# Second expert products of the last unit as three 16-bit products, with the splits on POOL and DVE

## The reference

```
x = x + 0.5 * ffn(layernorm(x))
x = x + attn(layernorm(x))
x = x + 0.5 * ffn(layernorm(x))
```

```
h = relu(einsum('ebnc,ech->ebnh', buf, W1) + b1)     # 128 -> 512
y = einsum('ebnh,ehc->ebnc', h, W2) + b2             # 512 -> 128
```

## Time and profile before

| | |
|---|---|
| median of 3 runs | 190.1 us (189.92 to 190.57) |
| the profiled execution | 190.01 us |
| its span, first to last instruction | 188.2 us |
| PE busy | 178.3 us (95%) |
| ACT busy | 150.9 us (80%) |
| DVE busy | 135.0 us (72%) |
| POOL busy | 66.1 us (35%) |
| granted TensorE clock | 1.0 in all slices |

### The profile page before, as it was taken

The page is one execution under the profiler, slowest core; times in us unless marked ns, Lnnn a source line. Parts: engine busy times, 40 slices in busy tenths (PEclk is TensorE's granted clock), DMA queues, the critical chain, the costliest instruction groups (busy, mean ns, idle before and its releaser), DMA issues.

```text
span 188.2 us, 5958 instructions
## 1 busy us (share of the span) xinstructions
PE 178.3 (95%) x2279; PEld 142.0 (75%) x2279; DVE 135.0 (72%) x402; ACT 150.9 (80%) x362; POOL 66.1 (35%) x106
## 2 busy tenths in 40 slices
PE   7998799999999999999999999898999999999991
PEld 7976798888978956654756565554699998999980
DVE  0998967957978799795557768799787785354254
ACT  3795999659869779999999999799887489885670
POOL 8924842000040007776654778579200000000000
PEclk9999999999999999999999999999999999999999
DMA  4999930360005999617875973704500008300303
GB/s 126 323 332 332 207 60 0 74 125 0 3 2 171 254 218 279 212 64 185 252 229 153 242 191 79 207 6 84 101 0 3 0 3 140 69 5 28 86 3 111
DMA packets 36460, 23.35 MB, mean 124 GB/s; under 512 B 16424, under 2 KB 33360, under 8 KB 36432
## 3 DMA queue, kind: packets, MB, share of 16 engines
q1 hardware_dynamic: 35744, 22.70, 48.4%
q10 hardware_dynamic: 688, 0.27, 0.5%
HBM read 14.05 MB, written 5.24 MB: 102 GB/s over the span
## 4 chain that ended last, share of the span: by engine, by line
PE 80%; DVE 13%; issue 4%; ACT 1%; DVEq 0%; POOL 0%; ACTq 0%; POOLq 0%
PE psB L1080 19%; PE psB L1155 7%; PE psS L960 5%; PE psS L962 5%; PE psS L961 5%; PE psB L1056 5%; PE psS L1138 4%; PE psB L970 4%; PE psB L1157 3%; PE psB L1047 3%; PE psB L1022 3%; DVE oh L860 2%; PE psB L1087 2%; PE psB L960 2%; PE psB L1176 2%
## 5 line engine op out<-in xcount | busy, mean ns | idle before, releaser
L604 POOL TENSOR_SCALAR_AFFINE_SELECT amat<-amat 128x512 f32<-128x512 f32 x64 | 44.7, 705 | 35.1 <-ACT amat L700 33.5
L700 ACT ACTIVATE amat<-psS 128x768 f32<-128x768 f32 x64 | 48.7, 815 | 3.1 <-PE psS L1140 2.3
L658 ACT ACTIVATE hid<-psS,biasT 128x160 f32<-128x160 f32 x128 | 39.4, 404 | 6.3 <-PE psS L962 5.5
L1080 PE MATMUL psB<-hid,w 128*128 128x160 f32 x256 | 39.6, 303 | 1.4 <-issue 1.3
L1080 PEld LDWEIGHTS psB<-hid,w 128*128 128x128 f32 x256 | 35.5, 190 | 2.5 <-issue 2.0
L960 PE MATMUL psS<-xe,w 128*128 128x160 f16 x128 | 27.1, 233 | 0.4 <-DVE xe L355 0.3
L962 PE MATMUL psS<-xe,w 128*128 128x160 f16 x128 | 27.1, 233 | 0.0
L961 PE MATMUL psS<-xe,w 128*128 128x160 f16 x128 | 27.1, 233 | 0.0
L670 ACT ACTIVATE yT<-psB,biasT 128x160 f32<-128x160 f32 (+1 forms) x32 | 13.4, 438 | 9.5 <-PE psB L1080 9.3
L1155 PE MATMUL psB<-amat,vst 128*32 128x256 f32 x256 | 20.3, 388 | 0.8 <-DVE x L929 0.7
L1138 PE MATMUL psS<-stack 64*128 64x256 f16 x128 | 15.9, 277 | 0.3
(11 more groups left out here) (157 smaller groups left out, 353.9 us busy)
## 6 DMA issues: line engine op xcount, KB each, us to landing
qk_parts<-qk SPq DMA_DIRECT2D x16, 256.0 KB, 3.1
stack<-qk_parts SPq DMA_DIRECT2D x16, 256.0 KB, 4.0
stack<-qk_parts SPq DMA_DIRECT2D x32, 128.0 KB, 3.8
amat<-in_L_ffn_W SPq DMA_DIRECT2D x8, 256.0 KB, 5.4
w<-in_L_ffn_W SPq DMA_DIRECT2D x8, 256.0 KB, 5.8
x<-in_L_attn_hidden_states SPq DMA_DIRECT2D x4, 256.0 KB, 4.5
out<-x SPq DMA_DIRECT2D x6, 128.0 KB, 1.9
ohT<-ohT SPq DMA_DIRECT2D x8, 64.0 KB, 2.7
```

The costliest lines, as they stand in the source:

```text
L604: pool.affine_select(out=d, in_=d, pattern=[[0, 2], [0, 2], [1, P]], compare_op=ALU.is_ge, fill=0.0, base=0, channel_multiplier=-1).then_i ...
L658: ins = act.activation(hid[:, n % 2, c, :], psS[:, wide_slot(s) + c // 2, (c % 2) * GS:(c % 2 + 1) * GS], ACT.Relu, bias=biasT[:, e * HC + ...
L700: act.activation(amat[:, n % A_RING, :, :], psS[:, wide_slot(s):wide_slot(s) + 2, 0:T + P], ACT.Square)\
L1080: ins = mm(bank(s)[:, 0:GS], w2[:, e, c, :], hid[:, n % 2, c, :], start=(c == 0), stop=(c == HC - 1))
```

## The change

The down stages of the last unit (1,1) are made as three 16-bit products, as the up stages are. Those of the other units stay 32-bit. For that

- POOL, after its last mask and after all `av` stages (`av_done`), walks the 8 experts: a copy of `w2[e]` (128x512) to 16 bits, a wait for it, and the subtraction; the parts go to `w2s`, which lies in `amat`, and `w2_split` counts.
- DVE has a new stage `hs.1.1.e`: it waits for the relu (`h_taken`), casts `hid` (128x640) to 16 bits, waits, and subtracts; the parts go to `hids`, in `stack`, and `h_split` counts.
- PE's down in the last unit waits for both, and issues 12 matmuls of 128x160 in 16 bits.
- All four lists are written anew, over the whole kernel, not only in the last unit.

The core of the diff:

```diff
@@ tiles
+        w2s = amat[:, :, :, :].rearrange("p s h c -> p (s h c)")[:, 0:E * HC * C].bitcast(f16).rearrange("p (a e h c) -> p a e h c", a=2, e=E, h=HC)
+        hids = stack[:, 0, :, :, :].rearrange("p s h t -> p (s h t)")[:, 0:4 * HC * GS].rearrange("p (n a h c) -> p n a h c", n=2, a=2, h=HC)
@@ gpsimd, after the masks
+            pool.wait_ge(av_done, B * HEADS // 4)
+            for e in range(E):
+                link(pool.tensor_copy(w2s[:, 0, e], w2[:, e]))
+                pool.tensor_tensor(w2s[:, 1, e], w2[:, e], w2s[:, 0, e], ALU.subtract).then_inc(w2_split, 1)
@@ vector
+                elif kind == "hs":
+                    up = ("up",) + s[1:]
+                    dve.wait_ge(h_taken, nth[up] + 1)
+                    full, parts = hid[:, nth[up] % 2], hids[:, nth[up] % 2]
+                    link(dve.tensor_copy(parts[:, 0], full))
+                    dve.tensor_tensor(parts[:, 1], full, parts[:, 0], ALU.subtract).then_inc(h_split, 1)
@@ tensor, down
-                    for c in range(HC):
-                        ins = mm(bank(s)[:, 0:GS], w2[:, e, c, :], hid[:, n % 2, c, :], start=(c == 0), stop=(c == HC - 1))
+                    if (l, g) == units[-1]:
+                        pe.wait_ge(w2_split, e + 1)
+                        pe.wait_ge(h_split, nth[("hs",) + s[1:]] + 1)
+                        for c in range(HC):
+                            for a, b in ((0, 0), (0, 1), (1, 0)):
+                                ins = mm(bank(s)[:, 0:GS], w2s[:, a, e, c, :], hids[:, n % 2, b, c, :],
+                                         start=(c + a + b == 0), stop=(c == HC - 1 and a == 1))
+                    else:
+                        for c in range(HC):
+                            ins = mm(bank(s)[:, 0:GS], w2[:, e, c, :], hid[:, n % 2, c, :], start=(c == 0), stop=(c == HC - 1))
```

More of the change, by code:

```diff
@@ new lines @@
+dph.0.1.0 dph.0.1.1 down.0.0.7 dph.0.1.2 dph.0.1.3 ex.0.1 up.0.1.0 yt.0.0.0 sq.0 yt.0.0.1 yt.0.0.2 wqkv
+down.0.1.0 up.0.1.1 up.0.1.2 ln1.1.0 down.0.1.1 down.0.1.2 up.0.1.3 up.0.1.4 down.0.1.3 qk.0.0.0 qk.0.0.1
+qk.0.1.0 qk.0.1.1 ln1.1.1 v.1 up.0.1.5 up.0.1.6 up.0.1.7 down.0.1.4 yt.0.1.0 down.0.1.5 down.0.1.6 down.0.1.7
+yt.0.1.1 qk.1.0.0 yt.0.1.2 qk.1.0.1 sc.0.0 qk.1.1.0 sc.0.1 sc.0.2 sc.0.3 qk.1.1.1 sc.0.4 v.2 sc.0.5 sc.0.6
+sc.0.7 ln1.1.2 sc.1.0 sc.1.1 xe.0.0 v.3 sc.1.2 sc.1.3 xe.0.1 sc.1.4 sc.1.5 sc.1.6 xe.1.0 sc.1.7 sc.2.0
@@ L134 @@
-qk.2.0.1 qk.2.1.0 qk.2.1.1 xe.2.0 xt.1.3 wo.0 v.5 ox.1 xe.2.1 qk.3.0.0 qk.3.0.1 qk.3.1.0 qk.3.1.1 wo.1 ox.2
-ln1.2.0 lnx.2.0 ox.3 wo.2 ln2.2.0 wo.3 ln1.2.1 xt.2.0 lnx.2.1 ln2.2.1 lg.1.0.0 ox.4 xt.2.1 lg.1.0.1 c1.1.0
-c2.1.0 xe.6.0 wo.4 ox.5 ps.1.0 xe.6.1 wo.5 ln1.2.2 ox.6 xe.7.0 lnx.2.2 xe.7.1 ln2.2.2 ox.7 wo.6 sm.1.0 xt.2.2
-wo.7 ln1.2.3 lnx.2.3 ln2.2.3 pw.1.0 lg.1.1.0 xt.2.3 lg.1.1.1 c1.1.1 c2.1.1 ps.1.1 dpl.1.1.0 dpl.1.1.1
-dpl.1.1.2 dpl.1.1.3 sm.1.1 yt.1.0.0 yl.1.0.0 yt.1.0.1 yt.1.0.2 yl.1.0.1 yl.1.0.2 pw.1.1 cb.1.0.0 yt.1.1.0
@@ L139 @@
-cb.1.0.1 cb.1.0.2 cb.1.0.3 yl.1.1.0 yl.1.1.1 yl.1.1.2 yl.1.1.3 yl.1.1.4 cb.1.1.0 cb.1.1.1 cb.1.1.2 cb.1.1.3
+dpl.0.1.2 dpl.0.1.3 pw.0.0 yt.0.0.0 sm.0.1 yl.0.0.0 yt.0.0.1 yt.0.0.2 yl.0.0.1 yl.0.0.2 pw.0.1 cb.0.0.0
+cb.0.0.1 ln1.1.0 cb.0.0.2 cb.0.0.3 lnx.1.0 ln2.1.0 xt.1.0 ln1.1.1 qk.0.0.0 qk.0.0.1 qk.0.1.0 qk.0.1.1 lnx.1.1
+ln2.1.1 v.0 yt.0.1.0 yl.0.1.0 xt.1.1 yt.0.1.1 yt.0.1.2 yl.0.1.1 yl.0.1.2 qk.1.0.0 qk.1.0.1 qk.1.1.0 cb.0.1.0
+qk.1.1.1 cb.0.1.1 ln1.1.2 cb.0.1.2 lnx.1.2 ln2.1.2 cb.0.1.3 ox.0 xt.1.2 v.4 qk.2.0.0 qk.2.0.1 ln1.1.3 qk.2.1.0
@@ new lines @@
+qk.2.1.1 lnx.1.3 ox.1 wo.0 xe.2.0 xe.2.1 v.5 wo.1 ln2.1.3 ln1.2.0 ox.2 xt.1.3 lnx.2.0 qk.3.0.0 qk.3.0.1 wo.2
+ox.3 qk.3.1.0 qk.3.1.1 ln2.2.0 wo.3 ln1.2.1 lnx.2.1 xt.2.0 ln2.2.1 ox.4 xt.2.1 lg.1.0.0 lg.1.0.1 c1.1.0 c2.1.0
+xe.6.0 ox.5 wo.4 ps.1.0 wo.5 xe.6.1 ln1.2.2 ox.6 lnx.2.2 xe.7.0 xe.7.1 sm.1.0 wo.6 ox.7 ln2.2.2 wo.7 ln1.2.3
+xt.2.2 lnx.2.3 pw.1.0 ln2.2.3 xt.2.3 lg.1.1.0 lg.1.1.1 c1.1.1 c2.1.1 ps.1.1 dpl.1.1.0 dpl.1.1.1 dpl.1.1.2
+dpl.1.1.3 yt.1.0.0 sm.1.1 hs.1.1.0 yl.1.0.0 hs.1.1.1 yt.1.0.1 yt.1.0.2 hs.1.1.2 hs.1.1.3 yl.1.0.1 yl.1.0.2
```

78 lines of the change are left out of this document (31 added, 47 removed).

## The result

The kernel before took 190.16 us (median of 20 executions), the changed kernel 190.91 us (20 executions): ratio 1.0035, 95% interval 1.002 to 1.005. So the change makes the kernel slower, by 0.2 to 0.5% (0.4 to 1.0 us). Measured once more beside the first experiments it took 190.46 us (10 executions) against 190.43 for the kernel before (25 executions), ratio 1.0011, interval 0.9991 to 1.0031, which does not exclude an equal time. Both intervals hold 0.2 to 0.3%, 0.4 to 0.6 us. Executions of one kernel scatter over about 1 us and crowd at both ends of it, so that a median depends on how many fell where; the fastest ones are 190.25 against 189.75 us in the first measurement and 190.36 against 189.73 in the second, 0.5 and 0.6 us apart. The loss is small, but it is there. 191.3 us had been forecast, between 188.8 and 193.0.

A forecast was written before the change was run, and what follows sets the result against it. The prediction took PE, busy without rest from 137 us on, to bound the kernel. It summed 190.0 - 2.1 (products) + 1.05 (last unit's chain) + 2.3 (POOL's split) = 191.3 us, range 188.8 to 193.0.

The forecast's parts named there:

- parts 1 and 2: Last unit: shorter 16-bit products take 2.1 us off PE, and the chain through DVE's splits takes 1.05 back.
- part 3: From 134 to 151 us, POOL's split of w2 holds up DVE's layer norm chain, so PE waits: 2.3 us, bounds 0 to 5.
- part 4: New lists from 0 to 134 us, no operation added or taken away: 0 us, within 0.7 either way.
- PE's time of the products: Last unit's eight downs: 0.83 us each as 16-bit products instead of 1.09, so 2.1 us leave PE.
- DVE's split of the relu output: Last unit: cast 0.52 and subtraction 0.75 us for each expert, 10.2 us in all, DVE about 20 busy us.
- The hand schedule of the last unit: New lists worked through from the start of up.1.1.0: PE's waits placed, down.1.1.7 ending at t = 19.2, 1.05 us left of 2.1.
- One sign of being wrong: The forecast is wrong if PE's gaps lie in the last unit and exceed 1.5 us there.
- The point from which it decides: PE waits once DVE's waits behind wo.7 exceed 1.8 us of filler plus what DVE idles.
- contention hidden: Rival: filler and DVE's idle time take up POOL's work from 134 us on, 189.0 us; chance 0.22.
- long POOL copy: Rival: contention from POOL's w2 split reaches the last router's selection and the one-hot builds, 193 to 195 us; chance 0.12.
- Partly hidden, 0.7 to 1.6 us of waits on PE: Rival: POOL's contention is only partly covered, 189.7 to 190.6 us, no change to tell; chance 0.20.
- The forecast's own case: PE waits for the layer norm chain that POOL holds up, 190.7 to 192.5 us; chance 0.40.

The follow-up runs named there:

- the first experiments: Four kernels taking the change apart: changed kernel again 190.46 us, new lists alone 191.38, everything but POOL's split 190.28, new lists with POOL's unread split 191.46.

## Why the prediction came out as it did

The time came out inside the range, and slower as forecast, but the term that carried the forecast was more than three times too high. In the prediction's own terms, by the profiles:

| term | forecast | measured |
|---|---|---|
| products and the chain in the last unit (parts 1 and 2) | -1.05 | -0.62 |
| POOL's split (part 3) | +2.3 | +0.69 |
| the new lists elsewhere (part 4) | 0, within 0.7 | +0.49 |
| sum | +1.25 | +0.56 |

The first measured term is the block of the last unit below, the second is PE's wait at `xt.2.3`, the third is what is left of 0.56.

- **PE's time of the products**: 0.83 us a down instead of 1.09, 2.1 us for eight. Right to the hundredth.
- **DVE's split of the relu output**: estimated 0.52 + 0.75 us by scaling the 512-column rows. Its rows show 0.49 and 0.83 us with starts 0.53 and 0.75 apart. Right.

```profile
168.26 0.82 DVE L910 TENSOR_TENSOR stack<-hid,stack 128x640 f16<-128x640 f32 x1
169.08 0.49 DVE L909 CAST stack<-hid 128x640 f16<-128x640 f32 x1
```

- **The hand schedule of the last unit**: waits of 0.74, 0.08, 0.22, 0.13 and 0.26 us were forecast at `up.1.1.2`, `down.1.1.0`, `.1`, `.4` and `.7`; 0.52, 0.20, 0.21, 0.42 and 0.37 were measured. All five places are right. The unit ended at t = 19.53 instead of 19.2 (161.25 to 180.78). `down.1.0.7` and the two transposes ahead of `up.1.1.0` took 1.16 and 0.94 us instead of 1.09 and 0.87, so the block is 21.63 us instead of 21.2, and saves 0.62 against the 22.25 of before instead of 1.05. `down.1.1.4` carries most of the error: from 162.3 to 175.3 us DVE's rows stand without a gap, so whatever I had too short on DVE since `down.1.1.0` adds up there (argued from the rows, not tested). One sign of being wrong that the prediction named did appear: more than 1.5 us of gaps in the last unit, 1.72 by distances of starts, more than twice PE's wait for the layer norm chain.
- **The lists elsewhere**, put at 0 within 0.7: 0.49, inside the bounds, but no zero. 0.12 lies ahead of `up.1.0.0`, 0.19 and 0.21 are the waits at `down.1.0.0` and `lg.1.1.1`. Alone the lists cost 0.93 us, because the wait at `up.1.1.2` is theirs too: the prediction had it in its last unit among the prices of the splits, and the kernel with the lists alone shows it without any split. That no operation is added or taken away was a reason for no change of PE's work, not of its waits.
- **POOL beside DVE**: the mechanism was right, and the size was 2.3 us where 0.69 was measured (0.67 between the kernels with and without it). This was the largest error, and the step of the prediction that failed. POOL's own rows came as taken (copy 0.61, subtraction 1.16, from 134.66 to 150.25). What failed is the count of waits on DVE. I let nearly every operation meet a fresh POOL operation. `sm.1.0` was to take 3.1 us; it took 1.9 (135.49 to 137.37), three of its five operations passing at their usual length, so `ox.7` was normalised by 138.83 and PE waited neither at `oT.7` nor at `xt.2.2`. The scalings were to wait 2.8 us; they waited 1.56 (2.68 less 1.12). The x split came at 149.24 instead of 150.4, and PE there at 148.7 instead of 149.0: 0.69 us of wait instead of 1.35.
- **The point from which it decides** (waits behind wo.7 over 1.8 us of filler plus DVE's idle time) held, and the kernel with the split under the old lists shows its other side: without the filler the four scalings waited 2.59 us, PE 4.8, and the clock added 1.6.
- **The rivals**: "contention hidden", 189.0, falls with the wait at `xt.2.3`; "long POOL copy" falls with the row of 0.61 us. "Partly hidden, 0.7 to 1.6 us of waits on PE", with 189.7 to 190.6 us and a chance of 0.20, is what happened: PE waited 0.69 us, and 190.0 + 0.56 is 190.6. The forecast's own case, 190.7 to 192.5, holds the median of the first measurement (190.91) and not that of the second (190.46). The total came as near as it did by luck: POOL's term was 1.6 us too high, and the last unit and the lists together 0.9 too low.

The Trainium skill, "SBUF — State Buffer", section "Who interferes with whom", has the rule on which the largest term stood, that VectorE and GpSimd block each other on their shared ports. The pair of kernels with and without POOL's split agrees: 2.68 against 1.12 us for the same four scalings. The Trainium skill's "GPSIMD Engine Reference", section "Engine selection", puts one-input work at roughly line rate, from which the estimate of 0.6 us for the copy was made; 0.61 was measured.

## What to carry to other kernels

Work given to an engine that idles is not free when it shares a resource with the engine that feeds the bound. Its price hangs on the slack of the chain just there: the same sixteen POOL operations cost 0.7 us under one order and 6.1 under another. With ten of them moved earlier they cost 3.7 us (176.01 us from the first move of `xe` to the last addition, against 172.35 without POOL's split) and 2.8 (175.18, with one more place of DVE's list changed). So price it in the schedule in which it will stand, and find first a stretch in which both the idle engine and its rival's critical chain have slack. And when a change comes with a reordered schedule, give the order alone a term of its own, and look in it for waits of the bounding engine: here it ate 0.93 of the 1.04 us that the shorter products had brought. The same products in an order that costs nothing (old lists up to `up.1.1.1`, no work of POOL) gained 1.35 us.

## What the runs showed of the hardware

- DVE and POOL take turns in both directions: POOL's copy, 0.61 us when alone, took 1.07 where DVE's subtraction was ahead of it.

```profile
140.18 1.07 POOL L614 CAST amat<-w 128x512 f16<-128x512 f32 x1
```
```profile
139.26 1.53 DVE L807 TENSOR_TENSOR xf<-xn,xf 128x512 f16<-128x512 f32 x1
```

  Read from the lengths: DVE's subtraction (0.69 us alone) waited for POOL's (begun 139.02, 1.21 us) until about 140.1, and POOL's next copy for DVE's until about 140.7.
- Small operations waited too: a cast of 128x64, 0.20 us alone (`p` at 163.03), took 0.49 beside POOL's split under the new lists, and 1.17 under the old ones. Beside the same split a sum over 128x64 and a reciprocal of 128x8 kept their 0.21 and 0.20 us.
- A pause of PE can cost twice: 1.8 us (with five experts split early) and 2.95 us (under the old lists) without a matmul were each followed by 6 us at a mean granted clock of 0.72, down to the level of 1.2 GHz, 1.5 to 1.6 us lost on top of the pause. At that level the products of an up started 0.13 us apart instead of 0.07. The clock fell after PE had begun again, not in the pause. Pauses of 0.54, 1.23 and 1.56 us were not followed by a lower clock.
